# Layer-0 attention: the P·V products of two images in one group of 36 key tiles instead of 12 and 24, with two places for the first 12 key tiles

## The reference

```python
x = x + _L0_conv_ref(_gn(x), ...)          # layer 0: 4 images, N = 2304 keys, 8 heads of 16 channels
# in it:
v = x @ Wv + bv
lepe = conv(v, dw_w) + dw_b                # 5 x 5 depthwise convolution
attn = einsum('bhnd,bhmd->bhnm', qr, kr) + mask          # mask: one N x N matrix per head
out = einsum('bhnm,bhmd->bhnd', softmax(attn), vr)
out = out + lepe
...
t = t + _L1_attn_ref(_ln_t(t), ...)        # layer 1: attention, then a routed feed-forward
t = t + _L1_ffn_ref(_ln_t(t), ...)
```

## Time and profile before

| what | us |
|---|---|
| median of three runs | 3687.6 (3686.34 to 3691.2) |
| the profiled execution | 3683.41 |
| its span, first to last instruction | 3681.3 |
| PE busy in the span | 3452.0 |
| DVE busy | 2688.0 |
| ACT busy | 2035.7 |
| POOL busy | 1626.9 |
| mean granted TensorE clock | 0.973 |

### The profile page before, as it was taken

How to read it: one execution, slowest core, us unless ns; L and a number is a source line. 1 busy time by engine, 2 the same in 40 slices (tenths; PEclk the granted TensorE clock), 3 DMA queues, 4 the chain that set the end, 5 groups by cost and what they waited for, 6 DMA issues and landing times. The chain is left out here.

```text
span 3681.3 us, 97035 instructions
## 1 busy us (share of the span) xinstructions
PE 3452.0 (94%) x30782; PEld 2666.7 (72%) x30782; DVE 2688.0 (73%) x6605; ACT 2035.7 (55%) x3641; POOL 1626.9 (44%) x822
## 2 busy tenths in 40 slices
PE   7649999999999999999999999999489999999989
PEld 4427777777777777777777777777367787878767
DVE  6858888888888888888888888888456564644457
ACT  3236666666666666666666666666345444455533
POOL 2336565566656656556656555665210000005012
PEclk8879999999999999999999999999799999999989
DMA  5434224224223322422422422222321020100011
GB/s 175 139 100 128 90 92 121 77 92 130 92 80 101 109 89 99 111 80 99 123 92 79 119 92 89 99 76 82 110 95 56 16 81 2 41 1 1 1 40 42
DMA packets 122674, 307.49 MB, mean 84 GB/s; under 512 B 15865, under 2 KB 85548, under 8 KB 101804
## 3 DMA queue, kind: packets, MB, share of 16 engines
q1 hardware_dynamic: 122540, 305.78, 26.7%
HBM read 251.43 MB, written 54.31 MB: 83 GB/s over the span
## 5 line engine op out<-in xcount | busy, mean ns | idle before, releaser
L729 DVE CUSTOM_DVE_ANT_0 c_S<-c_Sps,mask_tiles 128x768 f32<-128x768 f32 x1728 | 1618.9, 956 | 431.7 <-PE c_Sps L780 391.1
L670 ACT ACTIVATE c_PT<-c_Tps 128x512 f32<-128x512 f32 x2592 | 1428.6, 604 | 871.8 <-PE c_Tps L791 809.2
L642 POOL TENSOR_SCALAR c_S<-c_S,c_row_max 128x2304 f32<-128x2304 f32 x576 | 1410.8, 2449 | 966.4 <-DVE c_row_max L740 966.4
L791 PE MATMUL c_Tps<-ident,c_S 128*128 128x128 f32 x10368 | 1399.0, 273 | 4.1 <-ACT c_PT L670 4.1
L791 PEld LDWEIGHTS c_Tps<-ident,c_S 128*128 128x128 f32 x10368 | 1225.9, 140 | 150.8 <-ACT c_PT L670 9.7
L780 PE MATMUL c_Sps<-c_K,c_Q 96*128 (+1 forms) x3456 | 853.4, 328 | 58.9 <-DMA c_Q<-q_parts 42.4
L804 PE MATMUL c_Ops<-c_PT,c_V 128*32 128x256 f32 x10368 | 619.1, 382 | 0.8 <-ACT c_PT L670 0.8
L804 PEld LDWEIGHTS c_Ops<-c_PT,c_V 128*32 128x32 f32 x10368 | 307.4, 109 | 243.7 <-issue 47.7
L780 PEld LDWEIGHTS c_Sps<-c_K,c_Q 96*128 96x128 bf16 x3456 | 314.7, 98 | 219.0 <-issue 144.2
L1295 DVE TENSOR_SCALAR_CACHE_REDUCE l_S<-l_Sps 128x384 f32<-128x384 f32 x432 | 240.6, 558 | 291.9 <-PE l_Sps L1143 264.9
L1063 ACT ACTIVATE ln2T<-l_Tps 128x384 f32<-128x384 f32 x432 | 196.6, 491 | 397.6 <-PE l_Tps L1164 397.6
(11 more groups left out here) (209 smaller groups left out, 1743.8 us busy)
## 6 DMA issues: line engine op xcount, KB each, us to landing
mask_tiles<-in_mask SPq DMA_DIRECT2D x144, 1152.0 KB, 7.6
numerators<-c_O SPq DMA_DIRECT2D x288, 64.0 KB
ln<-numerators SPq DMA_DIRECT2D x8, 2304.0 KB, 8.5
q_parts<-f_parts SPq DMA_DIRECT2D x12, 576.0 KB, 3.4
k_parts<-f_parts SPq DMA_DIRECT2D x12, 576.0 KB
c_Q<-q_parts SPq DMA_DIRECT2D x72, 96.0 KB
c_K<-k_parts SPq DMA_DIRECT2D x8, 864.0 KB, 8.6
c_vpad<-v_padded SPq DMA_DIRECT2D x8, 756.0 KB, 14.8
```

Source lines behind the costliest of these rows:

```text
L642: pool.tensor_scalar(S[:, slot, :], S[:, slot, :], -1.0, row_max[:, slot:slot + 1], ALU.mult, ALU.add).then_inc(shifted, 1)
L670: act.activation(dst, src, ACT.Exp, scale=-1.0).then_inc(exp_done, 1)
L729: dve.tensor_tensor_reduce(out=S[:, r % ROW_SLOTS, cols(CH, c)].rearrange("p (k n) -> p k n", k=2), in0=Sps[:, n % S_SLOTS, :, 0:GW], in1= ...
L791: last = pe.transpose(Tps[:, g % T_SLOTS, cols(P, k)], S[:, (2 * b + t) % ROW_SLOTS, cols(P, kt)], ident[:, :])
```

## The change

The two value groups become one of 36 key tiles. It is issued in images 0 and 2 (for the pair before), after A1. `PT` gets two places for key tiles 0 to 11 of the even images, used in turn by `half`, and one for the rest, so that ACT can write the first three exponential groups of the next pair before the values of the last are done; it waits for `pt_used` at group 3 (`EARLY // 4`) of an even image alone. `PT` grows from 36 to 48 tiles. The transposes and scores are put in a new order around it, and the taps move to (3, 1), (5, 2) and (7, 1): after A1 of image 0, after A2 of image 1 and after A1 of image 2.

```diff
@@ -490,13 +490,14 @@
 
     with ExitStack() as ctx:
         sb, ps = buffers(nc, ctx, "c")
+        EARLY = 12
         sem = sem_maker(nc, ctx, "c")
         K = sb("K", [KR, 2 * B * N], BF16)
         Q = sb("Q", [KR, 2, B, 2 * P], BF16)
         S = sb("S", [P, 4, N])
         part_max = sb("part_max", [P, 4, NCH])
         row_max = sb("row_max", [P, 4])
-        PT = sb("PT", [P, 2, TILES, 2 * P])
+        PT = sb("PT", [P, 2 * EARLY + (TILES - EARLY) + TILES, 2 * P])
         V_next = sb("V_next", [P, B * TILES, D])
         V = sb("V", [P, B * TILES, 2 * D])
         O = sb("O", [P, 2, B, 2 * P])
@@ -522,11 +523,9 @@
         PAIRS = HEADS * HEAD_PAIRS
         ROWS = 2 * B
         CONV_STEPS = TAP_SLOTS + 1
-        TAP_AFTER = ((1, 2), (3, 0), (7, 0))
+        TAP_AFTER = ((3, 1), (5, 2), (7, 1))
         COLS = 4
         STORES = COLS + 1
-        V_TILES = [range(0, 3 * COLS), range(3 * COLS, 2 * TILES)]
-        V_GROUPS = len(V_TILES)
         FULL = [[(t, kt) for kt in range(first, first + 4)] for t in range(2) for first in range(0, TILES - 2, 4)]
         SPLIT = [(t, kt) for t in range(2) for kt in range(TILES - 2, TILES)]
         T_GROUPS = FULL[:4] + [SPLIT] + FULL[4:]
@@ -536,6 +535,12 @@
         S_SLOTS, T_SLOTS, O_SLOTS = 2, 3, 1
         ROW_SLOTS = 4
         LEAD = ROW_SLOTS - 1
+
+        def pt_place(half, image, kt):
+
+            if image:
+                return EARLY + TILES + kt
+            return half * EARLY + kt if kt < EARLY else EARLY + kt
 
         block = ctx.enter_context(nc.Block())
 
@@ -655,23 +660,23 @@
             def exp(ip, b):
 
                 for g, group in enumerate(T_GROUPS):
-                    if b % 2 == 0 and g in (0, 3):
-                        act.wait_ge(pt_used, V_GROUPS * (B // 2 * ip + b // 2) + 1 + g // 3)
-                    if b % 2 and g == 0:
-                        act.wait_ge(pt_used, V_GROUPS * (B // 2 * ip + b // 2 + 1))
+                    if b % 2 == 0 and g == EARLY // 4:
+                        act.wait_ge(pt_used, B // 2 * ip + b // 2 + 1)
                     act.wait_ge(t_ready, TG * (B * ip + b) + (g + 1 + TG * ROW_SLOTS // 2))
                     if group is SPLIT:
-                        dst = PT[:, b % 2, TILES - 2:TILES, :].rearrange("p k (t q) -> p t k q", t=2)
+                        place = pt_place(b // 2, b % 2, TILES - 2)
+                        dst = PT[:, place:place + 2, :].rearrange("p k (t q) -> p t k q", t=2)
                         src = Tps[:, g % T_SLOTS, :].rearrange("p (t k q) -> p t k q", t=2, k=2)
                     else:
                         t, first = group[0]
-                        dst = PT[:, b % 2, first:first + 4, cols(P, t)]
+                        place = pt_place(b // 2, b % 2, first)
+                        dst = PT[:, place:place + 4, cols(P, t)]
                         src = Tps[:, g % T_SLOTS, :].rearrange("p (k q) -> p k q", q=P)
                     act.activation(dst, src, ACT.Exp, scale=-1.0).then_inc(exp_done, 1)
 
             def take_o(ip, p, half):
 
-                act.wait_ge(pt_used, V_GROUPS * (B // 2 * ip + half + 1 + 1))
+                act.wait_ge(pt_used, B // 2 * ip + half + 1 + 1)
                 if half == 0:
                     act.wait_ge(o_stored, 16 * STORES * (ip + 1))
                     alone(act)
@@ -765,7 +770,7 @@
         @block.tensor
         def _(pe):
             pe.sem_inc(t_ready, TG * ROW_SLOTS // 2)
-            pe.sem_inc(pt_used, V_GROUPS)
+            pe.sem_inc(pt_used, 1)
             pe.sem_inc(o_taken, O_SLOTS)
 
             def scores(ip, p, r, c):
@@ -791,17 +796,16 @@
                     last = pe.transpose(Tps[:, g % T_SLOTS, cols(P, k)], S[:, (2 * b + t) % ROW_SLOTS, cols(P, kt)], ident[:, :])
                 last.then_inc(t_ready, 1)
 
-            def values(ip, half, group):
-
-                if group == 0:
-                    pe.wait_ge(o_taken, 2 * ip + half + 1)
-                    pe.wait_ge(v_placed, 2 * (ip // HEAD_PAIRS) + half + 1)
-                pe.wait_ge(exp_done, TG * (B * ip + 2 * half + (2 if group else 1)) + T_SLOTS)
-                for i in V_TILES[group]:
+            def values(ip, half):
+
+                pe.wait_ge(o_taken, 2 * ip + half + 1)
+                pe.wait_ge(v_placed, 2 * (ip // HEAD_PAIRS) + half + 1)
+                pe.wait_ge(exp_done, TG * (B * ip + 2 * half + 2) + T_SLOTS)
+                for i in range(2 * TILES):
                     j = i % COLS
                     kt, image = i % TILES, i // TILES
                     b = 2 * half + image
-                    last = pe.matmul(Ops[32 * j:32 * (j + 1), image, :], V[:, b * TILES + kt, :], PT[:, image, kt, :],
+                    last = pe.matmul(Ops[32 * j:32 * (j + 1), image, :], V[:, b * TILES + kt, :], PT[:, pt_place(half, image, kt), :],
                                      start=kt < COLS, stop=kt >= TILES - COLS)
                 last.then_inc(pt_used, 1)
 
@@ -815,37 +819,42 @@
                         elif not end:
                             scores(ip + 1, 1 - p, r - ROWS, c)
 
-                    def behind(group):
+                    def behind():
                         if b:
-                            values(ip, b // 2 - 1, group)
+                            values(ip, b // 2 - 1)
                         elif not start:
-                            values(ip - 1, 1, group)
+                            values(ip - 1, 1)
 
                     transposes(ip, b, 0)
                     ahead(0)
                     transposes(ip, b, 1)
                     if b % 2 == 0:
-                        behind(1)
                         ahead(1)
+                        behind()
+                        ahead(2)
                         transposes(ip, b, 2)
                         transposes(ip, b, 3)
-                        ahead(2)
                         transposes(ip, b, 4)
                         ahead(3)
+                        transposes(ip, b, 5)
+                        transposes(ip, b, 6)
+                        ahead(4)
+                        transposes(ip, b, 7)
+                        ahead(5)
+                        transposes(ip, b, 8)
                     else:
                         transposes(ip, b, 2)
                         ahead(1)
                         transposes(ip, b, 3)
                         transposes(ip, b, 4)
                         ahead(2)
-                        values(ip, b // 2, 0)
+                        transposes(ip, b, 5)
                         ahead(3)
-                    transposes(ip, b, 5)
-                    transposes(ip, b, 6)
-                    ahead(4)
-                    transposes(ip, b, 7)
-                    ahead(5)
-                    transposes(ip, b, 8)
+                        transposes(ip, b, 6)
+                        transposes(ip, b, 7)
+                        ahead(4)
+                        transposes(ip, b, 8)
+                        ahead(5)
 
             for r in range(LEAD):
                 for c in range(NCH):
@@ -857,8 +866,7 @@
                     pair(i * 2 + p, p)
             pair(PAIRS - 2, 0)
             pair(PAIRS - 1, 1, end=True)
-            for group in range(1, V_GROUPS):
-                values(PAIRS - 1, 1, group)
+            values(PAIRS - 1, 1)
 
 
 def layer1_attention(nc, a, s, ident, conv_bias, x1, ln2, ln2T, sums):
```

## The result

The changed kernel takes 3752.3 us (median of four runs, 3748.13 to 3752.37) against 3687.24 us before (four runs on the same chip): a ratio of 1.0172, 95% interval 1.0154 to 1.0189. It is slower by 65 us; 3775 was forecast, with a range of 3742 to 3812.

The account below looks back on a forecast made before the run. PE was taken as the bound of layer-0 attention. Stalls of 124.6 + 22.0, less 34.6 and 25.6 saved, plus 1.4 at the end, gave +87.8 on 3683.41, so 3771.2; the runs' median 4.2 higher, 3775; range 3742 to 3812.

Parts of the forecast that it names:

- What bounds the kernel, and where: Layer-0 attention: PE is the bound, and new waits for DVE's chunks at A5, A0 and A1 add PE time every pass.
- The saving of one group: Values: one group of 36 costs 4.02 us and saves 0.24 per pair of images, 34.6 us in all.
- Rival 2: Values: merging the groups saves nothing because cost goes by matmuls, giving 3810 us; chance 0.08.
- The old stall of 0.36 in image 3: A5 of image 3: the present wait goes as image 3 loses its tap, saving 0.36 x 71 = 25.6 us.
- Image 1, 1.73 us: Image 1: A5 1.45 late, A0 0.17 and A1 0.11 more, 1.73 us per pass, 124.6 us in all.
- Image 3, 0.31: Image 3 without a tap: A0 0.20 and A1 0.11 late, 0.31 us per pass, 22.0 us in all.
- The taps inside the values cost nothing: Two taps after A1 take 1.34 us each inside the 4.02 us of values, costing PE nothing; cover some 1.5 us.
- Rival 1: A5 of image 1: tap stays covered, giving 3627 us; decides if new stalls stay below 0.84 per pass; chance 0.08.
- Rival 3: PE clock in the attention stage: new waits make it fall, adding 73 us, 3848 in all; chance 0.07.
- Rival 4: 36-tile values: they wait for the Ops copy or exponentials, taking back the saving; 3790 to 3810 us; chance 0.02.
- How waits are counted: PE stalls: differences of starts are the measure, not the idle column, which shows 0.20 us for a stall of 0.36.
- the forecast by the column, 3729: Whole kernel, stalls sized by the idle column alone: a cost of 0.57 us per pass, 41 us, giving 3729.

Follow-up runs that it names:

- e6: Changed kernel with scores reordered so no two short steps adjoin, and taps after (3, 0), (3, 1), (7, 0): 3631.61 us, ratio 0.9844.
- e7: Changed kernel with two taps moved from (3, 1) and (7, 1) to (3, 0) and (7, 0), tap at (5, 2) kept: 3749.63 us, ratio 1.0163.
- e8: Kernel before with the tap after (1, 2) moved to (5, 2), the 12-tile value group still behind A2: 3669.95 us, ratio 0.9948.

## Why the prediction was right, and by how much not

- **What bounds the kernel, and where**: right. What is added is idle time of PE in front of A5, A0 and A1, at DVE's pace, but for one late transpose group in every second pass (see image 3).
- **The saving of one group**: right in size. 36 key tiles were put at 4.02 and took 4.02. By the prediction's terms the distance between groups without a stall is 16.18 - 0.24 = 15.94; e6 shows 15.93. Rival 2 falls.
- **The old stall of 0.36 in image 3**: gone, as predicted.
- **Image 1, 1.73 us**: the term that was mis-sized. From A2 to A1 it is 5.69 against 4.29, a stall of 1.40. Of the 0.33, 0.24 is the step from chunk A2 to the tap, taken as 1.12 from a row of the kernel before that held the first tap of a pass; the second tap of a pass starts after 0.88. The rest lies in A0 and A1, which started 1.01 and 1.02 after the start of the chunk before the last instead of 1.10. 0.33 x 72 = 24 us covers the whole distance between 3775 and 3752.3.
- **Image 3, 0.31**: by the distances 16.26 on average less 15.95, 0.31, but the agreement is luck. Where the distance is 16.18, A0 and A1 are 0.12 and 0.11 late, 0.23 against the 0.31 forecast: A0 came 1.66 after A4, not 1.74. Where it is 16.34, T0 is 0.28 late (1330.38 - 1329.77 - 0.33), A0 0.05 and the values 0.08, 0.4 in all. These are the passes in which PE's loop, of two passes, begins anew; the prediction has no term for it, and what makes T0 late was not separated.
- **The taps inside the values cost nothing**: right, e7; but their length of 1.34, taken from a tap with no shift beside it, was wrong by a factor of two, and 0.64 us of DVE's idle time was left behind the tap instead of the "some 1.5 us" of cover. It was no part of this kernel's time.
- **Rival 1** (the tap stays covered) is what e8 shows for the order with V12 (e6, in which next to nothing waits, comes to 3631.61, near this rival's 3627), and it failed here at the place and by the point named: 1.71 us of stalls per pass against 0.84. **Rival 3**: the clock is 1.00 in the window with PE busy 96.5%; the swing that the Trainium skill tells of (TensorE: Matmul & The Clock Gate, "A second HAM failure mode: psum-queue depth-cycling") didn't come with a wait of 1.1 us per pass. **Rival 4**: neither V36 nor the transposes wait for anything in each pass; the late T0 in every second pass is the exception. Before had it too, 0.12 late at the same place (16.65 against 16.54).
- **How waits are counted**: the starts were the right measure. The idle column has 73.6 + 28.5 = 102 us; by starts the stalls are (1.40 + 0.31) x 72 = 123. With these 123 the sum is 123 - 34.6 - 25.6 + 1.3 = +64 us, and +65 were measured; with the column's own figures, before and after, it is 102 - 13.2 - 34.6 + 1.3 = +56. The totals alone wouldn't have told: the forecast by the column, 3729, misses 3752.3 by as much as 3775 does.

## What to carry to other kernels

When a block of work is taken out of a list in order, ask what it covered on the other engine: V12 cost PE 1.44 us and gave DVE the time for a tap of 1.34, and taking it out of image 1 bought 0.24 us and cost 1.40 of waiting. With two slots, the sum of any two steps of the producer has to reach the consumer's start, its length and the way back (here 0.64 + 1.10 = 1.74 for two steps by the rows of before, and 1.66 where two short steps followed each other in the changed kernel), so short steps are put singly between long ones and the consumer's extra work behind the producer's longest block. A saving that ends in a loss can be kept if both repairs are made: the order and the taps of e6 turn +1.7% into -1.6%.

## What the runs showed of the hardware

The tap on DVE, which reads two tensors in SBUF, and POOL's shift hold each other up when they run at the same time, though they work on different tensors, and the one that comes second pays. Alone the tap takes 1.41 us and the shift 2.19.

- Tap first, the shift 0.25 behind it: the tap took 1.41 and the shift 3.21 (before, e6, e7, e8). The kernel before has such pairs in each pass; they make the mean of 2446 ns for a shift.
- Both within 0.03 of each other (first tap of a pass in e6, e7, e8): the tap took 1.42 and the shift 3.38 to 3.43 in most passes; in a few of e6 and e8 it was the other way round, the shift 2.19 and the tap 3.37.
- Shift first: the shift stayed at 2.2 and the tap took 2.69 to 2.79 where 1.5 to 1.6 us of the shift were still to come, 2.40 with 1.19 to come and 1.74 with 0.54 to come. In each case the tap ends 1.20 after the shift does, 0.2 less than its own 1.41: it hardly moves until POOL is done. Beside the last 0.11 us of a shift it isn't longer at all.

The chunk instruction, which reads one of its inputs from PSUM, shows no such effect: it takes 0.95 to 0.96 beside a shift and without one.

The Trainium skill (SBUF — State Buffer, "SBUF: two separate sides") says that GpSimd and a Vector instruction with two SBUF inputs take a shared pair of ports as a lock for a whole instruction and that the later one is blocked; by that rule, the runs agree for both orders, and a tap of 1.41 behind 1.59 us of shift would end at 3.0, where 2.79 was measured. The port itself no run here shows.
